# Later maxima in the second turn of a two-layer transformer kernel on Trainium2

## Chip, core and metric

The kernel runs on one core of a Trainium2 chip. Such a core has a tensor engine for matrix products (PE in the profile), a vector engine (DVE), a scalar engine for activations (ACT), a general engine (POOL, GpSimd) and a small engine that here only issues transfers (SP). Each works through a list of instructions of its own, in order, and waits on semaphores where it needs another's result. The metric is the time of one execution on the device in microseconds; lower is better.

## What is computed

Two transformer layers over an input of 8 batches, 512 tokens and 128 channels. In each, attention and a feed-forward net stand side by side on the same normalized input:

```python
xn = layernorm(x)
x  = x + attn0(xn) + ffn0(xn)    # ffn0: gate, up and down products, values rounded to fp4 by blocks of 16
xn = layernorm(x)
x  = x + attn1(xn) + moe(xn)     # moe: a shared net, and 2 of 8 experts for each token
```

Attention has 16 heads of 8 channels and a softmax over 512 keys. In both layers the kernel computes the scores twice: once roughly, for the maximum of each row, and once in full with that maximum folded in, for the exponentials.

## The kernel before

**Turns and slots.** The work on a batch is divided into turns of 16 slots. `turn_a(b)` runs layer 0's attention for batch b, `turn_b(b)` runs layer 1's attention for batch b − 1; they alternate: `turn_a(0)`, `turn_b(0)`, `turn_a(1)`, and so on. In slot k a turn computes two pairs of scores (`score_pair`, L387, lines L395) on the tensor engine, their exponentials on the scalar engine (`exponentials`, L753), and a slot later the sums with the values (`weighted_sums`, L383). All other work is hung into the slots by hand: `work_a` and `work_b` stand in each engine's program and name the slot and the place in it, "a" behind the first pair of scores, "b" behind the second, and on the vector engine "m" and "c" behind the slot's maxima.

**Maxima.** The attention of a later turn needs the maxima of its rows. They come in 16 units, u = 0 to 15. A unit is four products of `km` and `qm` on the tensor engine (L364) and two reductions of 128x1024 numbers on the vector engine (L1037). `units_a` and `units_b` (L254, L262) say which units stand in which slot; the maxima of a slot stand behind place "b" and before the sums. In `turn_a(1)` these are layer 1's maxima of batch 0, one unit a slot. Unit 4g is the first that needs group g of `qm[1]` and `km[1]` (`maxima`, L360). When units 0 to 7 are reduced, `max_rows(1, 0, 0)` turns them into rows: four transpositions (L285) into the ring, a cast on the scalar engine (L763), a subtraction on the vector engine (L1042), and on SP four small transfers (`load_rows`, L1601). The second half follows in slot 1 of the next turn.

**Banks.** All scores, maxima and some other products share three double banks (`mx`, L195, taken in turn by `to_pair`). A fourth pair waits until the first of the three before has been read. Single products and transpositions have one bank, the ring (`to_ring`), so each waits until the one before it has been copied out or read.

**What stands at the start of `turn_a(1)`.** In slot 0 place "b", `norm0(2)`; in slot 1 place "a", `max_rows(0, 1, 1)`; in slot 2, `q0(2)` at place "a" and `k0(2)` at "b" (L290). The scalar engine copies each out twice (`qk_out`, L725, lines L732 and L733), into `parts` and `qk_f`. Before that it waits until all transfers have landed that read `parts` for the batch and layer before.

**What stands at its end.** Slot 11 to 13, place "a": three groups of transpositions (`ffn_hidden`); slot 12 place "b", `gates_transposed`; slot 14 place "a", `ffn_down` (L352); slot 15 place "a", `shared_out` (L469). On the vector engine the steps of `quantize_x` stand in slots 11 to 13, and additions of the results of `ffn_down` and `shared_out` (L1031, L1130) in slots 14 and 15.

**SP's order** around the change: `store_early(1, 0)` (parts to `scratch`, L1562), `load_max(1, 0)` (`scratch` to `qm` and `km`, eight transfers, L1583), `store_late(1, 0)` (more of `scratch` and `rest`, L1568 to L1573), `load_stacks(1, 0, 0)`, `load_rows(0, 1, 1)`, `load_stacks(1, 0, 1)`, the same chain of stores and loads for layer 0's batch 2, then `load_rows(1, 0, 0)` and `load_stacks(0, 2, 0)`.

Of the kernel before, what the change touches and what calls it, by code (L numbers as in the profile page):

```python
# [28 lines left out]
SLOTS = 16  # L29
# [8 lines left out]
PLANE = B * T + 1  # L38
FIRST_TILE = 6
FIRST_UNITS = 10  # L40
NTILE = 2 * B * T // TS + E - 1
WROW = FE + EC * P + EC
NW = 4
# [46 lines left out]
def two_layers(nc, x, w_qkv, w_out0, b_out0, w_gate, w_up, w_down, wqT, wkT, wvT, woT, bq, bk, bv, bo,  # L90
               wr1, br1, wr2, br2, w1s, b1s, w2s, wmoe, b2, scratch, rest, xsort, y2, base, out):
    ctx = ExitStack()
    with ctx:
# [21 lines left out]
        iota8, ebase = sb("iota8", [P, E]), sb("ebase", [P, E])  # L115
        iota_t, token = sb("iota_t", [P, NTILE]), sb("token", [P, NT])
        minus_half = sb("minus_half", [P, NT])
# [58 lines left out]
        aside = sb("aside", [P, NTILE, 2])  # L176
        y_row = sb("y_row", [P, NTILE, 2], I32)

# [74 lines left out]

        def units_a(b, k):  # L254

            if b >= 1:
                return [(1, b - 1, k)]
            if k < SLOTS - FIRST_UNITS:
                return [(0, 0, FIRST_UNITS + k)]
            return [(0, 1, k - 8)] if k >= 8 else []  # L260
# [15 lines left out]
        def _(pe):  # L276
# [221 lines left out]
            def work_a(b, k, place):  # L498

                at = (k, place)  # L500
                if b <= LAST:
                    if at == (1 if b else 6, "a"):
                        max_rows(0, b, 1)
                    if at == (11, "a"):
                        ffn_hidden(b, 0)
                    if at == (12, "a"):
                        ffn_hidden(b, 1)
                    if at == (13, "a"):
                        ffn_hidden(b, 2)
                    if at == (14, "a"):  # L510
                        ffn_down(b)
                if 1 <= b < LAST:
                    if at == (0, "b"):
                        norm0(b + 1)
                    if at == (2, "a"):
                        q0(b + 1)
                    if at == (2, "b"):
                        k0(b + 1)
                if b >= 2:
                    if at == (3, "a"):  # L520
                        sums_transposed(1, b - 2, 0)
                    if at == (4, "a"):
                        sums_transposed(1, b - 2, 2)
                    if at == (5, "a"):
                        attention_transposed(1, b - 2)
                    if at == (6, "a"):
                        attention_out(1, b - 2)
                if b >= 1:
                    if at == (5, "b"):
                        v1(b - 1)  # L530
                    if b - 1 < LAST:
                        if at == (3, "b"):
                            router_hidden(b - 1)
                        if at == (4, "b"):
                            router_logits(b - 1)
                        if at == (10, "a"):
                            ranks(b - 1)
                        if at == (12, "b"):
                            gates_transposed(b - 1)
                    if at == (7, "b"):  # L540
                        shared_hidden(b - 1, 0)
                    if at == (8, "b"):
                        shared_hidden(b - 1, 1)
                    if at == (9, "a"):
                        max_rows(1, b - 1, 0)
                    if at == (15, "a"):
                        shared_out(b - 1)
# [112 lines left out]
            quantized_x(0)  # L660
            for u in range(FIRST_UNITS):
                if u == 1:
# [42 lines left out]
        def _(act):  # L705
# [78 lines left out]
            def work_a(b, k, place):  # L784
                at = (k, place)
                if b <= LAST:
                    if at == (1 if b else 6, "a"):
                        max_rows(0, b, 1)
                    if at == (8, "b"):
                        sums_out(0, b, 0)  # L790
                    if at == (11, "a"):
                        copy_out(("hT", b, 0), hqT[:, 0, :])
                    if at == (12, "a"):
                        copy_out(("hT", b, 1), hqT[:, 1, :])
                    if at == (13, "a"):
                        copy_out(("hT", b, 2), hqT[0:FC[2][1], 2, :], rows=FC[2][1])
                if 1 <= b < LAST:
                    if at == (0, "b"):
                        copy_out(("xT0", b + 1), xnT[0][:, :])
                    if at == (2, "a"):  # L800
                        qk_out(0, b + 1, 0)
                    if at == (2, "b"):
                        qk_out(0, b + 1, 1)
                if b >= 2:
                    if at == (0, "b"):
                        sums_out(1, b - 2, 1)
                    if at == (5, "a"):
                        copy_out(("aT", 1, b - 2), attT[:, :])
                if b >= 1:
                    if b - 1 < LAST:  # L810
                        if at == (3, "b"):
                            router_hidden(b - 1)
                        if at == (6, "a"):
                            router_exp(b - 1)
                        if at == (9, "b"):
                            router_tanh(b - 1)
                        if at == (12, "b"):
                            copy_out(("wT", b - 1), w9T[:, :], rows=E + 1)
                    if at == (7, "b"):
                        shared_hidden(b - 1, 0)  # L820
                    if at == (8, "b"):
                        shared_hidden(b - 1, 1)
                    if at == (9, "a"):
                        max_rows(1, b - 1, 0)

            def work_b(b, k, place):
# [96 lines left out]
        def _(dve):  # L923
# [286 lines left out]
            def work_a(b, k, place):  # L1210

                at = (k, place)
                if b <= LAST:
                    if at == (1 if b else 6, "a"):
                        max_rows(0, b, 1)
                    if at == (5, "c"):
                        quantize_h(b, 1, 0)
                    if at == (6, "m"):
                        quantize_h(b, 1, 1)
                    if at == (7, "m"):  # L1220
                        quantize_h(b, 1, 2)
                    if at == (7, "c"):
                        quantize_h(b, 1, 3)
                    if at == (14, "a"):
                        ffn_down(b)
                if 1 <= b < LAST:
                    if at == (4, "c"):
                        split_second(0, b + 1)
                    if at == (5, "m"):
                        split_third()  # L1230
                if b + 1 <= LAST:
                    if at == (11, "c"):
                        quantize_x(b + 1, 0)
                    if at == (12, "m"):
                        quantize_x(b + 1, 1)
                    if at == (12, "c"):
                        quantize_x(b + 1, 2)
                    if at == (13, "m"):
                        quantize_x(b + 1, 3)
                if b >= 2:  # L1240
                    if at == (3, "a"):
                        sums_divided(1, b - 2, 0)
                    if at == (4, "a"):
                        sums_divided(1, b - 2, 2)
                    if at == (6, "a"):
                        add_projection(1, b - 2)
                if b >= 1:
                    if at == (5, "b"):
                        values1(b - 1)
                    if b - 1 < LAST:  # L1250
                        if at == (4, "b"):
                            router_sort(b - 1)
                        if at == (6, "c"):
                            router_choice(b - 1)
                        if at == (8, "m"):
                            router_hits(b - 1)
                        if at == (8, "c"):
                            gate_difference(b - 1)
                        if at == (10, "b"):
                            places(b - 1)  # L1260
                        if at == (11, "m"):
                            router_weights(b - 1)
                    if at == (9, "a"):
                        max_rows(1, b - 1, 0)
                    if at == (15, "a"):
                        shared_out(b - 1)
# [107 lines left out]
            for n in (1, 2):  # L1374
                dve.drain()
                quantize_weights(n)
            for u in range(FIRST_UNITS):
                if u == 6:
# [384 lines left out]
```

## Time and profile before

| | |
|---|---|
| median of 3 runs | 1481.52 us (1475.12 to 1487.46) |
| the profiled execution | 1481.92 us |
| its span, first to last instruction | 1480.2 us |
| mean granted clock of the tensor engine | 0.906 of 2.4 GHz |

The profile is one execution. It gives each instruction its start, its duration and its line; where an engine stood idle before an instruction, it names what ended the wait. A page sums this up for the whole span. A table of waits adds up who waited for whom in a stretch; a timeline lists the instructions of an engine in order, neighbours of one kind merged (x2, x4), with the idle time before them in square brackets; a table of windows gives for chosen stretches each engine's busy time and the granted clock.

### The profile page before, as it was taken

The page shows a single profiled execution, that of the slowest core. Times are in us where ns is not written, and L with a number is a line of the kernel's source. Part 1 is how long each engine was busy: PE and PEld are TensorE (multiplying, and loading weights), DVE is VectorE, ACT ScalarE, POOL GpSimd, SP SyncE. Part 2 cuts the span into 40 slices and gives each one's busy share as a digit, 9 for nine tenths or more (in the row PEclk, how much of TensorE's full clock was granted, in tenths as well). Part 3 has the DMA queues.
Part 4 walks back from the last instruction along what each step waited for, and adds up shares of the span by engine and source line. Part 5 has one row for each costly group of instructions (what it writes and reads, how often), then busy time and mean ns, then how long its engine had stood idle before and what let it go on. Part 6 is the DMA issues. An engine that isn't in the chain of part 4 may idle for free.

```text
span 1480.2 us, 19496 instructions
## 1 busy us (share of the span) xinstructions
PE 1173.5 (79%) x6807; PEld 513.0 (35%) x6807; DVE 949.7 (64%) x1600; ACT 789.5 (53%) x1011; POOL 454.5 (31%) x409
## 2 busy tenths in 40 slices
PE   2588588887988798779877987798789746988895
PEld 1213224322432243124322431243124224778841
DVE  7857576787677767776777677767784353622323
ACT  1254265766476657665666576657666512233364
POOL 9621424232423232223222322231221211344420
PEclk9768798999799999988998999989989857999997
DMA  5512172136213611351145113511420074455544
GB/s 156 127 54 48 44 187 74 33 92 160 60 33 93 172 47 34 117 148 48 34 114 150 48 34 111 146 48 33 115 52 14 21 187 115 145 171 177 178 147 128
DMA packets 149507, 144.12 MB, mean 97 GB/s; under 512 B 13689, under 2 KB 141890, under 8 KB 149410
## 3 DMA queue, kind: packets, MB, share of 16 engines
q1 hardware_dynamic: 143922, 132.96, 33.2%
q0 software_dynamic: 4544, 9.38, 2.0%
q8 instruction: 54, 0.88, 0.3%
q10 hardware_dynamic: 944, 0.54, 0.1%
q14 instruction: 43, 0.35, 0.1%
HBM read 90.19 MB, written 52.12 MB: 96 GB/s over the span
## 4 chain that ended last, share of the span: by engine, by line
PE 40%; DVE 19%; ACT 13%; DMA 7%; issue 6%; DVEq 5%; SPq 5%; POOL 2%; ACTq 0%; POOLq 0%
DVE nm L1037 13%; PE sums L383 8%; PE mx L395 7%; ACT ex L753 5%; PE mx L364 5%; PE mx L485 3%; PE mx L494 3%; PE ring L290 2%; PE ring L295 2%; ACT L753 2%; PE ring L469 2%; DMA ks<-xsort 2%; DVEq L971 1%; DMA qs<-xsort 1%; PE ring L285 1%
## 5 line engine op out<-in xcount | busy, mean ns | idle before, releaser
L1037 DVE TENSOR_REDUCE nm<-mx 128x2 f32<-128x1024 f32 x512 | 601.7, 1216 | 165.5 <-PE mx L364 164.5
L753 ACT ACTIVATE ex<-mx 128x1024 f32<-128x1024 f32 x512 | 511.5, 1024 | 333.0 <-PE mx L395 331.6
L395 PE MATMUL mx<-qs,ks 128*128 128x512 bf16 (+1 forms) x1024 | 324.6, 414 | 73.6 <-DVE nm L1037 29.2
L383 PE MATMUL sums<-ex,vs 128*18 128x512 f32 x2048 | 295.1, 649 | 1.7 <-ACT ex L753 1.5
L395 PEld LDWEIGHTS mx<-qs,ks 128*128 128x128 bf16 (+1 forms) x1024 | 76.4, 101 | 369.4 <-issue 157.1
L364 PE MATMUL mx<-km,qm 32*128 32x512 bf16 x1024 | 143.8, 418 | 59.2 <-DVE nm L1037 26.8
L1445 POOL TENSOR_TENSOR parts<-qk_f,parts 128x512 bf16<-128x512 f32 x32 | 36.9, 1175 | 293.5 <-DVE parts L956 293.5
L1453 POOL TENSOR_SCALAR binade<-binade 128x704 f32<-128x704 f32 (+1 forms) x24 | 56.3, 2347 | 198.5 <-DVE binade L988 198.5
L364 PEld LDWEIGHTS mx<-km,qm 32*128 32x128 bf16 x1024 | 36.9, 93 | 207.3 <-issue 91.5
L1416 POOL TENSOR_TENSOR rstd<-veps,minus_half 128x4 f32<-128x4 f32 x16 | 16.8, 1047 | 247.8 <-DVE veps L947 247.8
L1478 POOL DMA_INDIRECT xsort<-xn,pos_i x64 | 62.6, 978 | 63.7 <-DVE pos_i L1124 46.5
L1485 POOL DMA_INDIRECT y<-qs,y_row x40 | 38.3, 957 | 107.8 <-DVE qs L1184 100.6
L383 PEld LDWEIGHTS sums<-ex,vs 128*18 128x18 f32 x2048 | 35.5, 98 | 74.7 <-issue 63.6
L753 ACT ACT_TABLE_LOAD x29 | 37.2, 1283 | 37.9 <-PE mx L395 37.9
L1456 POOL TENSOR_TENSOR h_sb<-h_sb,binade 128x704 f32<-128x704 f32 x32 | 53.5, 1672 | 2.6
L1485 POOL DMA_INDIRECT y<-ks,y_row x38 | 36.4, 957 | 49.9 <-DVE ks L1184 44.1
L1042 DVE TENSOR_TENSOR nm_hl<-ring,nm_hl 8x512 bf16<-8x512 f32 x32 | 22.2, 695 | 42.6 <-ACT nm_hl L763 42.6
L780 ACT ACTIVATE work<-mx,qs 128x256 f32<-128x256 f32 x40 | 15.7, 474 | 52.2 <-PE mx L485 52.2
L445 PE MATMUL mx<-xnT,w_sb 128*128 128x512 f32 x64 | 33.4, 648 | 5.3 <-DVE nm L1037 5.2
L469 PE MATMUL ring<-w_sb,hs 128*128 128x128 f32 x256 | 36.2, 285 | 0.0
L1184 DVE COPY qs<-mx 128x256 f32<-128x256 f32 x20 | 8.5, 425 | 42.3 <-PE mx L494 42.3
L757 ACT COPY pv_sb<-sums 128x512 f32<-128x512 f32 x32 | 18.7, 586 | 30.5 <-PE sums L383 30.0
(212 smaller groups left out, 1569.5 us busy)
## 6 DMA issues: line engine op xcount, KB each, us to landing
scratch<-parts SPq DMA_DIRECT2D x128, 256.0 KB, 3.7
ks<-scratch SPq DMA_DIRECT2D x64, 256.0 KB
qs<-scratch SPq DMA_DIRECT2D x64, 256.0 KB
qs<-wmoe SPq DMA_DIRECT2D x20, 514.0 KB, 3.7
ks<-wmoe SPq DMA_DIRECT2D x19, 514.0 KB, 3.6
qm<-scratch SPq DMA_DIRECT2D x64, 128.0 KB, 2.6
km<-scratch SPq DMA_DIRECT2D x64, 128.0 KB, 2.6
rest<-parts SPq DMA_DIRECT2D x32, 128.0 KB, 3.3
```

The costliest lines, as they stand in the source:

```text
L364: done = pe.matmul(bank[:, j, :], qm[l][r, g, t * P:(t + 1) * P], km[l][r, g, :], start=True, stop=True)
L383: done = pe.matmul(acc[32 * j:32 * j + 2 * VW, :], values[:, start:start + 2 * VW], ex[:, s % NEX, j, :], start=q == 0 and t == 0, stop=q ...
L395: done = pe.matmul(bank[:, j, :], ks[l][r, h, t * P:(t + 1) * P], qs[l][r, h, :], start=True, stop=True)
L469: pe.matmul(bank[:, t * P:(t + 1) * P], hs[:, c, t * P:(t + 1) * P], w2_sb[:, c, :], start=c == 0, stop=False)
L485: done = pe.matmul(bank[:, c // 2, c % 2 * TS:(c % 2 + 1) * TS], wbuf[i % NW][:, c * P:(c + 1) * P], xgT[i % 2], start=True, stop=True)
L494: done = pe.matmul(bank[:, 0, h * P:(h + 1) * P], hm[i % 2][:, c, h * P:(h + 1) * P], wbuf[i % NW][:, FE + c * P:FE + (c + 1) * P], start= ...
L753: act.activation(ex[:, s % NEX, 2 * i:2 * i + 2, :], bank[:, :, :], ACT.Exp, scale=SCALE).then_inc(free, 1)
L1037: dve.tensor_reduce(nm[l][:, t, h:h + 2], bank[:, :, :], AX.X, ALU.max, negate=True).then_inc(free, 1)
L1453: pool.tensor_scalar(e2d, e2d, 1.0, 1.5 * 2.0 ** 22, ALU.max, ALU.mult).then_inc(rounded, 1)
L1456: pool.tensor_tensor(d, d, e2d, op).then_inc(rounded, 1)
L1478: pool.indirect_dma_start(out=xsort[:, :], out_offset=bass.IndirectOffsetOnAxis(ap=pos_i[:, b, c, t:t + 1], axis=0), in_=xn[1][:, t, :], i ...
L1485: pool.indirect_dma_start(out=y2[:, :], out_offset=bass.IndirectOffsetOnAxis(ap=y_row[:, i, h:h + 1], axis=0), in_=yo[i % 2][:, h * P:(h + ...
```

## The change

In `turn_a(1)` the units start in slot 3 instead of slot 0. Slots 3 to 12 have one unit each (0 to 9), slots 13, 14 and 15 two each (10 and 11, 12 and 13, 14 and 15). Unit 7 now stands in slot 10, so `max_rows(1, 0, 0)` stands in slot 11 instead of slot 9 in the three programs that contain it (PE, ACT, DVE); in slot 11 it comes behind `ffn_hidden(1, 0)`, which has the same place. No other turn changes, and SP's and POOL's programs remain as they are.

```diff
+FIRST_SHIFT = 3
...
         def units_a(b, k):
 
+            if b == 1:
+                first, last = FIRST_SHIFT, SLOTS - FIRST_SHIFT
+                return [(1, 0, u) for u in ([k - first] if first <= k < last else [2 * k - SLOTS, 2 * k - SLOTS + 1] if k >= last else [])]
             if b >= 1:
                 return [(1, b - 1, k)]
...
-                    if at == (9, "a"):
+                    if at == (11 if b == 1 else 9, "a"):
                         max_rows(1, b - 1, 0)
```

The last two lines stand alike in the programs of the tensor, scalar and vector engine.

## Rows read from the trace of the kernel before

**Rows 1.** Page: the span; busy us, share of span, instructions of each engine.
```profile
span 1480.2 us, 19496 instructions
...
PE 1173.5 (79%) x6807; PEld 513.0 (35%) x6807; DVE 949.7 (64%) x1600; ACT 789.5 (53%) x1011; POOL 454.5 (31%) x409
```

**Rows 2.** Timeline, tensor engine, slot 0: start, us, line, count, [idle before, releaser].
```profile
184.24 0.61 PE L364 MATMUL mx<-km,qm 32*128 32x512 bf16 x4 [10.07 <-DMA km<-scratch]
```

**Rows 3.** Timeline of SP's queue: first load, first and last late stores.
```profile
180.96 0.60 SPq L1583 DMA_DIRECT2D qm<-scratch  x1
...
186.12 0.59 SPq L1568 DMA_DIRECT2D scratch<-parts  x1
...
188.32 2.00 SPq L1573 DMA_DIRECT2D rest<-parts  x2
```

**Rows 4.** Timelines of the vector and scalar engines ahead of slot 2's copies.
```profile
179.19 0.53 DVE L988 TENSOR_SCALAR binade<-h_sb 128x704 int32<-128x704 int32 x1
...
192.56 0.59 ACT L732 CAST parts<-ring 128x512 bf16<-128x512 f32 x1 [1.29 <-DMA rest<-parts]
```

**Rows 5.** Timeline of the tensor engine, slot 2: q0, k0, the unit.
```profile
189.99 1.02 PE L290 MATMUL ring<-xnT,wqkv_sb 128*128 128x512 f32 x2
...
193.69 1.13 PE L290 MATMUL ring<-xnT,wqkv_sb 128*128 128x512 f32 x2 [2.24 <-ACT qk_f L733]
194.75 0.39 PE L364 MATMUL mx<-km,qm 32*128 32x512 bf16 x4
```

**Rows 6.** Windows: stretch, length; PE, PEld, DVE, ACT, POOL; PE clock; DMA, GB/s.
```profile
76.50:86.00 9.50, 9.50 (x34) 1.60 (x32) 4.71 (x4) 4.19 (x5) 1.40 (x2) 0.50 0.18 54
...
177.00:187.00 10.00, 2.76 (x12) 1.06 (x12) 4.53 (x7) 1.17 (x3) 8.05 (x5) 0.60 0.63 187
...
193.70:200.00 6.30, 6.30 (x36) 1.40 (x36) 3.92 (x4) 4.42 (x6) 0.00 (x0) 1.00 0.78 188
```

**Rows 7.** Timeline of the scalar engine in `turn_a(0)`: exponentials of three successive slots.
```profile
85.61 1.94 ACT L753 ACTIVATE ex<-mx 128x1024 f32<-128x1024 f32 x2 [2.66 <-PE mx L395]
90.20 1.94 ACT L753 ACTIVATE ex<-mx 128x1024 f32<-128x1024 f32 x2 [2.65 <-PE mx L395]
93.28 1.94 ACT L753 ACTIVATE ex<-mx 128x1024 f32<-128x1024 f32 x2 [1.15 <-PE mx L395]
```

**Rows 8.** Timelines of three engines: slot 9's row of maxima; slots 11, 12.
```profile
225.51 1.06 PE L285 MATMUL ring<-ident,nm 128*8 128x128 f32 x4
...
228.68 0.68 DVE L1042 TENSOR_TENSOR nm_hl<-ring,nm_hl 8x512 bf16<-8x512 f32 x1 [1.88 <-ACT nm_hl L763]
...
236.84 0.66 PE L395 MATMUL mx<-qs,ks 74*128 74x512 bf16 x2
...
237.21 0.58 ACT L717 COPY hqT<-ring 128x512 f32<-128x512 f32 x1
...
237.86 2.35 DVE L1037 TENSOR_REDUCE nm<-mx 128x2 f32<-128x1024 f32 x2 [2.34 <-PE mx L364]
...
239.21 0.60 PE L285 MATMUL ring<-ident,h_sb 128*128 128x128 f32 x4
```

**Rows 9.** Timeline of the vector engine, slots 13 to 15.
```profile
246.08 2.35 DVE L1037 TENSOR_REDUCE nm<-mx 128x2 f32<-128x1024 f32 x2
...
249.45 0.69 DVE L1031 TENSOR_TENSOR acc<-acc,ring 128x512 f32<-128x512 f32 x1 [0.51 <-PE ring L352]
...
257.55 0.69 DVE L1130 TENSOR_TENSOR macc<-macc,ring 128x512 f32<-128x512 f32 x1 [4.97 <-PE ring L470]
```

**Rows 10.** Timeline of the tensor engine: slots 14, 15, and the next turn's start.
```profile
246.13 0.60 PE L395 MATMUL mx<-qs,ks 128*128 128x512 bf16 x2
246.57 2.84 PE L352 MATMUL ring<-wdT,hqT 128*128 128x128 f32 x24
...
251.09 0.61 PE L395 MATMUL mx<-qs,ks 128*128 128x512 bf16 x2
...
259.29 1.04 PE L395 MATMUL mx<-qs,ks 74*128 74x512 bf16 x4
```

More of the change, by code:

```diff
@@ L822, in work_a @@
                         shared_hidden(b - 1, 1)
-                    if at == (9, "a"):
+                    if at == (11 if b == 1 else 9, "a"):
                         max_rows(1, b - 1, 0)
@@ L1262, in work_a @@
                             router_weights(b - 1)
-                    if at == (9, "a"):
+                    if at == (11 if b == 1 else 9, "a"):
                         max_rows(1, b - 1, 0)
```

## Prediction

> **What bounds the kernel now.** I read the page first: the tensor engine is busy for 79% of the span, the vector engine for 64%, so no engine is full and the waits decide [rows 1]. Then I read the timelines of layer 0's second turn, engine by engine, for what stands idle and what ends each wait.
>
> The turn ends at 259.3 us [rows 10]. In the old order its slot 0 asks at once for layer 1's first maxima, and the tensor engine stands for 10.07 us until `km` has landed, at 184.24 [rows 2]. That is the hole the change is aimed at. But the timeline of the SP queue shows a second transfer behind the first. SP issues the early stores, then the eight loads of `qm` and `km` from 180.96, then only at 186.12 the late stores, the last two from 188.32 for 2.00 us [rows 3]. ScalarE's `qk_out(0, 2, 0)` in slot 2 waits for just these late stores, because `parts` may not be overwritten earlier. It waits 1.29 us, for `rest`, and starts at 192.56 [rows 4]. The tensor engine has issued `q0` at 189.99, and its next product of that kind, `k0` of slot 2, needs the one ring bank back: it starts at 193.69 after 2.24 us of idling [rows 5]. So two waits stand one behind the other, and the second ends 9.5 us after the first (193.7 − 184.2). In those 9.5 us the old kernel does the maxima of units 0 and 1.
>
> **The change, part by part.**
>
> *Slots 0 to 2 lose their units.* Slots 0 and 1 have scores, one transposition and the sums; nothing there waits for `km`. The vector engine is done with its own work of the turn before at 179.19 + 0.53 = 179.7 [rows 4], then does the maxima's rows of slot 1, and frees the ring at about 180.5; `q0` runs there, a good 9 us before its old 189.99. ScalarE then meets the late stores. Their time is made by the vector engine's split, GpSimd's third part and SP's own order, and none of these waits for a unit of maxima. They land at 192.5 as before, so `k0` starts at 193.7 as before. What is behind ScalarE's wait: its exponentials of slot 2's second half, its copy of `k0`, hence the ring, hence the tensor engine. The 10.07 us therefore return as a wait of about 12 us at `k0` (181.5 to 193.7). Gained is only the unit of slot 2 behind it: its four products are 0.39 us [rows 5]. I take −0.4; the bounds are 0 and −9.5 (the latter if the late stores came early, a rival below).
>
> *The clock behind the hole.* In the old trace the stretch with the 10 us hole, 177 to 187, was granted 0.60 of full speed, a mixture of 1.2 and 2.4 GHz, and 193.7 to 200 the whole 2.4 GHz [rows 6]: the slow part fell into the hole and into the products that still had the second wait before them. Now the engine stands until 193.7, and the slow part falls on slots 2 and 3, which nothing covers. What a slot costs at 1.2 GHz is shown by the turn before: at a granted 0.50 [rows 6] the exponentials of successive slots start 4.59 us apart (85.61 to 90.20), just after it 3.08 us (90.20 to 93.28) [rows 7]; 1.5 us a slot. Between no such slot and four (twice the two that fit into the 9.5 us of that stretch) I take one, +1.5; bounds 0 and +6. Of the clock the Trainium skill (TensorE: Matmul & The Clock Gate, Part 1, "What's actually happening") says that the throttled rate is the default and that activity releases it. [...] Were the rule not to hold here, the sum would be 1.5 us less, 1489.7.
>
> *Slots 3 to 12 keep one unit each*, with the same neighbours; nothing changes but the unit's number, so 0.
>
> *The row of maxima moves from slot 9 to slot 11.* In slot 9 little comes back: its four transpositions take 1.06 us [rows 8], but they lie beside exponentials which the same slot must wait for. In slot 11 they come behind `ffn_hidden`, in the same place "a", and there is one ring bank: the transpositions wait for ScalarE's copy of `hqT` (237.21 + 0.58), then take 0.60 us as the others do at 2.4 GHz, and the second pair of scores, before at 236.84, starts at about 238.3 (+1.4). ScalarE casts (0.6 us), the vector engine subtracts (0.68 us) and only then reduces the slot's unit: at about 239.8, before at 237.86, +2.0 [rows 8]. The vector engine has no idle time left in slots 12 and 13, so these 2.0 us stay. Bounds 0 and 2.3. SP issues this row's four loads two slots later, and the stacks of batch 2 queued behind them come later too; they are wanted a whole turn later, so this is free.
>
> *Slots 13 to 15 take two units each.* Three units are six reductions more; a pair of them is 2.35 us [rows 9]: 7.05 us. How much of it is hidden, step by step, with the 2.0 us carried in:
> - Slot 13: the four reductions run from 248.1 (before: two from 246.08) to 252.8. There are three double banks for scores and maxima. The first score pair of slot 14 follows four pairs of maxima and needs the bank of the second, read at 250.5; before it started at 246.13 [rows 9, 10]. +4.4.
> - Slot 14: `ffn_down` (2.84 us, from 246.57 before) ends at 253.7, its addition at 254.4; four reductions to 259.2. The first score pair of slot 15 needs the second of them, at 256.8, and follows the sums: 257.0 against 251.09, +5.9 [rows 9, 10].
> - Slot 15: `shared_out` follows, with those scores as long as before (251.1 to 257.5): to 263.4. The vector engine idled 4.97 us in front of its addition [rows 9]; slot 14's last reductions now fill half of that. The addition ends at 264.2, four reductions at 269.0.
> - Next turn: its first scores, before at 259.29 [rows 10], need the second of the four, 266.7, and the third, 267.9. GpSimd's rounding of `xq`, started 4.4 us later, is still earlier than its reader. I carry +8.2 for this part and the one before together.
>
> Bounds for the two together: if all idle time of the vector engine there were filled (0.51 + 4.97 [rows 9]), 7.05 − 5.5 = +1.6; if none, 7.05 + 2.3 = +9.4. I stay near the upper end because the order within a slot is fixed: slot 15's units stand behind `shared_out`, so they can't fill the idle time in front of it.
>
> **Sum.** −0.4 + 1.5 + 8.2 = +9.3 us. The profiled execution took 1481.92 us around a span of 1480.2 [rows 1], 0.4 us above the median of the runs (1481.52): 1481.9 + 9.3 = 1491.2, so 1491. Behind this turn every stage follows in a chain through the tensor and vector engines and begins 8 to 10 us later, and nothing gives that back.
>
> **Rivals.**
> 1. *Not slower: the tail takes the units in.* The idle time of slots 13 to 15 is filled, +1.6, with nothing for the clock: 1481.9 − 0.4 + 1.6 = 1483; with a slot 9 that gives its 1.06 us back, 1482. For it: the vector engine's 4.97 us of idle time. Against it: three banks and the fixed order. It decides if the first scores of slot 15 start less than 2 us later than before, counted from slot 3.
> 2. *Faster: the second wait isn't there.* If the late stores landed about 9.5 us earlier, `k0` would follow `q0` at once and the head gains 9.5: 1481.9 − 9.5 + 8.2 = 1481 with the full tail, 1474 with a tail of 1.6. For it: the wait seen in the old trace is only 1.29 us long. Against it: it is short because the first wait hides it; its end, 192.56, stands where SP's queue puts it.
> 3. *Slower by more: the clock.* Four slots at 1.2 GHz instead of one: 4 × 1.5 − 1.5 = 4.6 more, 1496; and if the small holes in the tail bring the low level there too, for one or two slots, 1498. For it: the hole now ends where the dense part begins. Against it: slots 3 to 8 partly wait for the vector engine, which has its own pace.
>
> **Chances.** The forecast, 1486 to 1495: 0.56. Rival 1, 1480 to 1486: 0.21. Rival 2, 1473 to 1480: 0.06. Rival 3, 1495 to 1503: 0.17. The runs of before lie between 1475.1 and 1487.5, 0.4% to either side, so about 1% is what can be told from no change: 1466.7 and 1496.3. Above 1496.3 lies most of rival 3 and the last edge of the forecast if the runs scatter upwards, 0.18. Below 1466.7 there is hardly a case, 0.03. The rest, 0.79, is within 1%. The range, 1479 to 1500, takes in rival 1 and most of rival 3 and leaves out rival 2 and the outer edges; the likeliest case's own range is 1486 to 1495.
>
> **What the profile after would show.** The wait of L364 for `km` is gone. ScalarE's wait at L732 for `rest` grows from 1.29 to some 11 us and still ends near 192.5; the tensor engine's wait at L290 grows from 2.24 to about 12 us and ends near 193.7. The granted clock behind 193.7 is below 1.0. The first scores of slot 15 and of the next turn come about 6 and 8 us later, with waits of L395 and L364 for the vector engine's L1037. It is wrong if L290's wait ends clearly before 193, or if the next turn starts within 3 us of 259.3.

## The result, and the profile after

The changed kernel takes 1497.39 us (median of 20 runs, 1485.96 to 1515.14), the kernel before 1482.87 us (20 runs, 1467.66 to 1492.82). The ratio is 1.0101, with a 95% interval of 1.0076 to 1.0126: one per cent slower, about 15 us (11 to 19). Medians take in all runs, ratios leave out those more than 1.5% above the fastest run of their kernel (three of these 20), and two of the profiled executions below, of the tail alone and of the changed kernel with another order of the stores, were such runs. The forecast was +9.3 us, 1491, within 1479 to 1500. The measured time lies in the wide range, above the 1486 to 1495 that was called likeliest: the direction and the place are right, the size is too small by a third.

The profiled execution of the changed kernel took 1492.52 us, 10.6 us more than the profiled one of before. Its page, the two lines that answer to [rows 1], shows the same busy times in a longer span:

```profile
span 1490.6 us, 19496 instructions
...
PE 1173.6 (79%) x6807; PEld 512.9 (34%) x6807; DVE 949.6 (64%) x1600; ACT 790.0 (53%) x1011; POOL 454.8 (31%) x409
```

No work was added, so all that was lost is waiting, or the tensor engine's clock. (In the changed kernel the line numbers behind `units_a` are 4 higher.) The hole first. The table of waits for 173 to 200 us (engine, line, what was waited for; us in total, times, the longest):

```profile
DVE nm L1041 <- PE mx L368: 21.2, 1, 21.2
...
PE ring L294 <- ACT qk_f L737: 12.9, 1, 12.9
ACT parts L736 <- DMA rest<-parts: 12.8, 1, 12.8
```

The wait of L364 for `km` [rows 2] is gone, and in its place stand the two that were small in [rows 4, 5]: ScalarE waits 12.8 us instead of 1.29 for the late stores, the tensor engine 12.9 us instead of 2.24 for the ring. The vector engine has nothing to reduce for 21.2 us. The tensor engine's timeline shows where the hole ends and what follows (start, us, line, count, idle time before):

```profile
177.79 1.10 PE L294 MATMUL ring<-xnT,wqkv_sb 128*128 128x512 f32 x2 [0.67 <-DVE nm_hl L1046]
178.73 0.60 PE L399 MATMUL mx<-qs,ks 74*128 74x512 bf16 x2
192.19 2.08 PE L294 MATMUL ring<-xnT,wqkv_sb 128*128 128x512 f32 x2 [12.87 <-ACT qk_f L737]
194.20 1.91 PE L387 MATMUL sums<-ex,vs 128*18 128x512 f32 x8
...
225.06 1.89 PE L399 MATMUL mx<-qs,ks 74*128 74x512 bf16 x4 [3.29 <-ACT hs L750]
...
238.30 1.01 PE L289 MATMUL ring<-ident,nm 128*8 128x128 f32 x4 [0.89 <-ACT hqT L721]
...
250.29 0.39 PE L368 MATMUL mx<-km,qm 32*128 32x512 bf16 x2 [1.00 <-ACT ex L757]
251.50 0.61 PE L368 MATMUL mx<-km,qm 32*128 32x512 bf16 x2 [0.83 <-DVE nm L1041]
252.04 1.91 PE L387 MATMUL sums<-ex,vs 128*18 128x512 f32 x8
253.89 1.03 PE L399 MATMUL mx<-qs,ks 128*128 128x512 bf16 x2
254.72 2.93 PE L356 MATMUL ring<-wdT,hqT 128*128 128x128 f32 x24
...
261.03 0.61 PE L399 MATMUL mx<-qs,ks 128*128 128x512 bf16 x2
...
270.93 0.61 PE L399 MATMUL mx<-qs,ks 74*128 74x512 bf16 x2
```

Of `q0` at 177.79 nothing is won, `k0` waits until 192.19 (193.69 in [rows 5]). `k0` then takes 2.08 us for what took 1.13, the sums 1.91 for 1.05: 1.2 GHz. The table of windows says the same of the stretches (start and end, length; PE, PEld, DVE, ACT, POOL busy; granted clock; DMA):

```profile
177.00:192.20 15.20, 1.66 (x6) 0.50 (x5) 0.65 (x2) 2.15 (x4) 7.28 (x4) 0.70 0.54 166
192.20:196.90 4.70, 4.70 (x13) 0.96 (x14) 0.00 (x0) 1.95 (x3) 0.00 (x0) 0.50 0.81 194
197.00:224.00 27.00, 20.93 (x121) 6.17 (x118) 22.24 (x40) 18.51 (x21) 6.71 (x5) 1.00 0.67 172
224.30:244.60 20.30, 17.59 (x68) 5.00 (x69) 12.67 (x24) 10.06 (x14) 10.46 (x10) 0.50 0.15 47
...
251.50:254.90 3.40, 3.40 (x13) 0.91 (x14) 3.34 (x3) 0.00 (x0) 0.00 (x0) 0.50 0.01 4
```

In [rows 6] the slow part lay in 177 to 187, and 193.7 to 200 had the full clock; now it lies behind the hole, in slots 2 and 3. And it stands twice in the tail: until 244.6, over slots 9 to 12, and from 251.5 to 254.9, in slot 13. The first of these is only partly new. The kernel before has a low stretch there too, but it ends at 237.0, early in slot 11; the 24 us from 235 on have a mean of 0.96, which is some 2 us at 1.2 GHz:

```profile
221.50:234.50 13.00, 9.60 (x41) 2.26 (x41) 10.13 (x20) 8.83 (x11) 6.02 (x5) 0.57 0.36 111
235.00:259.00 24.00, 23.05 (x164) 12.82 (x160) 14.98 (x23) 11.69 (x14) 11.99 (x11) 0.96 0.24 59
```

The vector engine in slots 11 to 15, beside [rows 8] and [rows 9]:

```profile
240.09 0.68 DVE L1046 TENSOR_TENSOR nm_hl<-ring,nm_hl 8x512 bf16<-8x512 f32 x1 [4.19 <-ACT nm_hl L767]
240.75 2.35 DVE L1041 TENSOR_REDUCE nm<-mx 128x2 f32<-128x1024 f32 x2
...
246.23 2.35 DVE L1041 TENSOR_REDUCE nm<-mx 128x2 f32<-128x1024 f32 x2 [1.55 <-PE mx L368]
...
250.23 4.61 DVE L1041 TENSOR_REDUCE nm<-mx 128x2 f32<-128x1024 f32 x4
...
257.69 0.69 DVE L1035 TENSOR_TENSOR acc<-acc,ring 128x512 f32<-128x512 f32 x1 [2.33 <-PE ring L356]
258.44 4.62 DVE L1041 TENSOR_REDUCE nm<-mx 128x2 f32<-128x1024 f32 x4
267.48 0.69 DVE L1134 TENSOR_TENSOR macc<-macc,ring 128x512 f32<-128x512 f32 x1 [4.42 <-PE ring L474]
268.35 4.62 DVE L1041 TENSOR_REDUCE nm<-mx 128x2 f32<-128x1024 f32 x4 [0.18 <-PE mx L368]
```

The twos stand there as groups of four reductions, 4.6 us each. In slot 11 the engine waits 4.19 us for the cast of the moved row; in front of the addition of `shared_out` it still waits 4.42 us, of 4.97 before.

To compare executions, the rest uses one ruler. A turn's length is counted from the end of the vector engine's split in the turn before (L956 of the kernel before; it lets the stores start) to the first exponential of the next turn's slot 1; within it, the start of ScalarE's copy of `q0` of batch 2 (L732, ended by the late stores' landing) and the first exponentials of the slots. All but the split's end are starts in the timelines of the vector and the scalar engine. The split's end differs by up to 5.9 us between the traces (169.9 to 175.8), from the first turns, which no kernel here changes; the ruler takes that out. From the copy of `q0` on:

| us | before | after | lost |
|---|---|---|---|
| copy of `q0` to slot 3 | 192.56 to 196.76: 4.20 | 191.07 to 197.13: 6.06 | 1.9 |
| slot 3 to slot 11 | to 236.29: 39.53 | to 236.66: 39.53 | 0.0 |
| slot 11 to 13 (moved row) | to 243.66: 7.37 | to 247.81: 11.15 | 3.8 |
| slot 13 to 14 | to 246.84: 3.18 | to 255.02: 7.21 | 4.0 |
| slot 14 to 15 | to 251.79: 4.95 | to 261.73: 6.71 | 1.8 |
| slot 15 to the next turn's slot 1 | to 263.47: 11.68 | to 275.52: 13.79 | 2.1 |
| sum | 70.91 | 84.45 | 13.5 |

13.5 us lost where 9.3 were forecast. Counted from the split it is 87.7 and 102.4, 14.7 us: in this execution the first loads were also issued 1.1 us later behind the split (6.4 us behind it, 5.2 before), which the other traces with this head and the old order of the stores don't show.

### The profile page after: what moved, and what is told of

It is laid out like the page before. It is cut to its first block, busy times and chain, and to the rows that moved or that the text cites. A ratio compares the mean times of both kernels' runs of the same rounds, so it can differ in the third digit from the quotient of the medians.

```text
span 1490.6 us, 19496 instructions
## 1 busy us (share of the span) xinstructions
PE 1173.6 (79%) x6807; PEld 512.9 (34%) x6807; DVE 949.6 (64%) x1600; ACT 790.0 (53%) x1011; POOL 454.8 (31%) x409
## 4 chain that ended last, share of the span: by engine, by line
PE 40%; DVE 20%; ACT 14%; issue 7%; DMA 7%; DVEq 5%; SPq 4%; POOL 2%; ACTq 0%; POOLq 0%
DVE nm L1041 14%; PE sums L387 8%; PE mx L399 7%; ACT ex L757 6%; PE mx L368 4%; PE mx L489 3%; PE mx L498 3%; PE ring L294 2%; PE ring L299 2%; DMA ks<-xsort 2%; ACT L757 2%; PE ring L473 2%; PE ring L289 1%; PE mx L449 1%; DVEq L975 1%
## 5 line engine op out<-in xcount | busy, mean ns | idle before, releaser
L294 PE MATMUL ring<-xnT,wqkv_sb 128*128 128x512 f32 x32 | 20.2, 716 | 22.1 <-ACT qk_f L737 20.7
```

Of the source, the lines that this page charges most:

```text
L294: pe.matmul(bank[0:rows, 0:width], lhsT, rhs, start=True, stop=True).then_inc(ring_full, 1)
```

## The experiments

The theory at this point had three parts: a head that only moves the hole from `km` to the late stores and pays for it with the clock; a moved row that costs 2 us or more; twos in the tail that cost the most. Its rivals were that one part, the head with its hole and clock above all, makes the whole loss. All ratios are to runs of the kernel before on the same chip; "turn" is the length by the ruler above, 87.7 us before.

### The row of maxima alone

```diff
-                    if at == (9, "a"):
+                    if at == (11 if b == 1 else 9, "a"):
                         max_rows(1, b - 1, 0)
```

> Only the row of maxima moves, from slot 9 to slot 11; the units stay one a slot from slot 0. Theory (three parts: a head that gains nothing, rows of maxima that cost 2 us in slot 11, twos in the tail that cost the most): slot 12's first scores come 1.5 to 4 us later against slot 10's than before, the whole is 1 to 4 us slower than before. Rival (the row's move makes most of the loss, because it holds the ring and the vector engine in a full slot): 8 to 12 us slower.

Measured: 1491.3 us, ratio 1.0048 (1.0015 to 1.0081). By this ratio the whole is 7 us slower (2 to 12): more than the theory said, less than the rival, and too wide an interval to choose. The turn chooses. It is 90.45 us, 2.7 longer, of which 1.97 lie between slots 11 and 13 (9.34 us for 7.37); the other 0.8 lie ahead of the copy of `q0`, where nothing was changed, and from slot 13 on all is as before. The vector and the tensor engine there:

```profile
238.35 0.60 PE L285 MATMUL ring<-ident,nm 128*8 128x128 f32 x4 [1.17 <-ACT hqT L717]
...
239.72 0.68 DVE L1042 TENSOR_TENSOR nm_hl<-ring,nm_hl 8x512 bf16<-8x512 f32 x1 [3.77 <-ACT nm_hl L763]
240.33 2.33 DVE L1037 TENSOR_REDUCE nm<-mx 128x2 f32<-128x1024 f32 x2
```

The transpositions wait for the copy of `hqT`, as reckoned, and the slot's unit starts 3.62 us behind the slot's first exponential (240.33 to 236.71) instead of 1.57 (237.86 to 236.29), 2.0 us later. The term of +2.0 us holds for the row alone. In the changed kernel the same stretch lost 3.8: there the four transpositions ran at 1.2 GHz, 1.01 us instead of 0.60, and the scores and sums up to slot 12 with them (the 224.3 to 244.6 window). That the clock makes the difference is seen in the other traces that have the row in slot 11: with the tail alone and with the stores' order changed the transpositions take 0.60 us and the stretch loses 1.97 too; with the hole filled it is at 1.2 GHz until 239.2, 7.9 us into slot 11, and loses 3.8.

### The head alone, with the twos early

```diff
+            if b == 1 and k < 6:
+                return [(1, 0, u) for u in ([2 * k - 6, 2 * k - 5] if k >= 3 else [])]
             if b >= 1:
                 return [(1, b - 1, k)]
```

> The head of the change without its tail: no units in slots 0 to 2, two each in slots 3, 4 and 5, one each from slot 6 on, the row of maxima in slot 9 as before. Theory (the head moves the hole to k0 and gains nothing; what costs is the tail's position): k0's wait at the ring is 12 to 13 us as in the changed kernel, the last slots are as before, the whole is 3 to 8 us slower than before. Rival (the loss comes with the hole at k0 and the low clock behind it, wherever the twos stand): 12 to 16 us slower, as the change itself.

Measured: 1499.62 us, ratio 1.0110 (1.0060 to 1.0160), 16 us slower, and that is what the rival said. The turn is 99.0 us, 11.3 longer; slots 11 to the next turn are as before to 0.02 us, so the whole loss lies between the copy of `q0` and slot 11. `k0` waited 11.78 us. The clock stayed low for much longer than in the changed kernel (the wait, then two windows):

```profile
187.92 2.07 PE L292 MATMUL ring<-xnT,wqkv_sb 128*128 128x512 f32 x2 [11.78 <-ACT qk_f L735]
...
177.00:187.90 10.90, 0.00 (x0) 0.00 (x0) 0.00 (x0) 1.11 (x3) 4.32 (x3) 0.50 0.70 209
188.00:200.80 12.80, 11.57 (x34) 2.01 (x36) 4.62 (x4) 4.48 (x6) 0.00 (x0) 0.50 0.81 174
```

So twos aren't cheap in early slots either, or the clock made it. The next two tell these apart.

### The hole filled

In slot 2 of the changed kernel, ahead of `k0`:

```diff
+            def fill():
+                bank, full = to_pair("fill")
+                r, h = score_rows(0), head(0, 2)
+                for n in range(48):
+                    done = pe.matmul(bank[:, n % 2, :], ks[0][r, h, 0:P], qs[0][r, h, :], start=True, stop=True)
+                done.then_inc(full, 1)
...
                    if at == (2, "b"):
+                        if b == 1:
+                            fill()
                         k0(b + 1)
```

(A copy on the vector engine that reads the bank is left out here; nothing uses its result.)

> The changed kernel with 48 extra products (bf16, 128x512, into a double bank that nobody else needs just then) on the tensor engine in the hole ahead of k0 of slot 2; their result is read by one tiny copy and not used. Theory (the hole at k0 costs twice: the wait itself, and 1.2 GHz in the slots behind it): k0 starts when it did against the stores' landing, runs at 2.4 GHz (1.05 us instead of 2.08), slot 3 starts 1.5 to 5 us earlier against it, and the whole is 2 to 5 us faster than the changed kernel. Rival (the low clock behind the hole is hidden by the vector engine's pace): 0 to 1 us.

Measured: 1500.3 us, ratio 1.0126 (1.0075 to 1.0176). In the trace:

```profile
177.22 10.52 PE L311 MATMUL mx<-qs,ks 74*128 74x512 bf16 x48
189.05 1.13 PE L294 MATMUL ring<-xnT,wqkv_sb 128*128 128x512 f32 x2 [1.30 <-ACT qk_f L746]
190.11 1.05 PE L394 MATMUL sums<-ex,vs 128*18 128x512 f32 x8
```

`k0` and the sums run at full clock, and from the copy of `q0` to slot 3 it takes 3.87 us (187.92 to 191.79): 2.2 less than in the changed kernel, and 0.33 less than before, which is the unit that slot 2 no longer has. This isolates the clock's price at this place, 2.2 us, and confirms the −0.4 of the sum. The tail, from slot 11 on, loses 11.6 us, as in the changed kernel (11.7). The time of the whole doesn't show the 2.2 us, and the 2 to 5 us of the theory aren't there: 2.2 us are 0.15%, less than half of the interval's half-width, and the whole can't decide on it.

The same filling in the kernel with the early twos:

> The kernel with the twos in slots 3 to 5 and the row of maxima in slot 9 (no units in slots 0 to 2), with the 48 extra products in the hole ahead of k0; their result is not used. Theory (of the 11 us that this kernel's turn lost against the stores' landing, the low clock behind the hole made some 3 to 5, the twos' vector work the rest): k0, the sums and the scores of slots 3 to 5 run at 2.4 GHz, the turn loses 6 to 8 us, the whole is 5 to 9 us slower than before. Rival (the twos alone make it, through banks and the vector engine): 10 to 12 us lost in the turn, clock or not.

Measured: 1494.27 us, ratio 1.0047 (1.0010 to 1.0083); the turn is 94.65 us, 6.9 longer, against 11.3 without the filling. From `q0`'s copy on it lost 82.13 − 77.85 = 4.3 us less. So the twos in slots 3 to 5 cost 7.3 us (slot 3 to 11 takes 46.80 us for 39.53), about three units of 2.35 us unhidden. The clock was full behind the hole until 204.5, where a stretch at 1.2 GHz to 207.9 began, in slots 4 and 5; what that adds wasn't separated. And the low clock behind an unfilled hole cost 4.3 us there and 2.2 in the changed kernel. The rival of the second experiment was right on its number, for two causes that add up.

### The tail alone

Units 0 to 2 in slots 0 to 2, none in slots 3 to 5, 3 to 9 in slots 6 to 12, then twos; the row in slot 11. In `units_a`, in place of the changed kernel's two lines:

```diff
+                if k < FIRST_SHIFT:
+                    return [(1, 0, k)]
+                first, last = 2 * FIRST_SHIFT, SLOTS - FIRST_SHIFT
+                return [(1, 0, u) for u in ([k - FIRST_SHIFT] if first <= k < last else [2 * k - SLOTS, 2 * k - SLOTS + 1] if k >= last else [])]
```

> The tail of the change without its head: units 0 to 2 in slots 0 to 2 as before, none in slots 3 to 5, units 3 to 9 in slots 6 to 12, two each in slots 13 to 15, the row of maxima in slot 11. Theory (the tail makes most of the loss): from slot 11 to the next turn 9 to 12 us are lost as in the changed kernel, slots 3 to 5 give 1 to 3 us back, the whole is 6 to 11 us slower than before. Rival (the head with its hole and clock makes it): 0 to 4 us slower.

Measured: 1496.01 us, ratio 1.0037 (0.9995 to 1.0080). By the ratio that is 5.5 us, between the two forecasts, and the interval includes no difference. The turn is 94.7 us, 7.0 longer, on the theory's side. The parts: slots 3 to 11 take 36.55 us, 3.0 less than before; slots 11 to 13 lose 2.0; slot 13 to the next turn takes 27.8 us, 7.9 more than the 19.8 of before. The changed kernel loses 7.9 there too (27.7), the filled one 7.8, the next experiment's 7.9. So the twos' price in the tail is the best known number here. It has a price of the clock in it: each of the five traces with twos in the tail has a short stretch at 1.2 GHz in slot 13 or between 13 and 14, and none of the nine others has one there. A unit taken out of slots 3 to 5 is worth 1.0 us, one out of the hole a tenth of a microsecond.

### The order of the stores

In the changed kernel, layer 1's late stores of batch 0 ahead of the loads:

```diff
                 store_early(1, b)
-                load_max(1, b)
-                store_late(1, b)
+                if b == 0:
+                    store_late(1, b)
+                    load_max(1, b)
+                else:
+                    load_max(1, b)
+                    store_late(1, b)
```

> The changed kernel, with layer 1's late stores of batch 0 issued ahead of the loads of qm and km instead of behind them. Theory (the hole at k0 is SP's order: the late stores stand behind eight loads that take 5 us to issue and wait for the early stores): ScalarE's wait for rest shrinks from 12.8 us to 4 to 6 us, k0 starts 6 to 9 us earlier, the whole is 5 to 9 us faster than the changed kernel, so still 5 to 10 us slower than before. Rival (the stores land late by themselves, for instance because the transfers share the engines): the wait stays above 10 us and the time is that of the changed kernel, some 14 us slower than before.

Measured: 1490.65 us, ratio 1.0029 (0.9994 to 1.0064), 0.7% below the changed kernel's ratio; the two intervals don't meet. Against before it is 4 us slower, and the interval includes no difference. SP, ScalarE and the tensor engine:

```profile
179.01 1.00 SPq L1577 DMA_DIRECT2D rest<-parts  x2
180.05 0.60 SPq L1587 DMA_DIRECT2D qm<-scratch  x1
...
183.02 0.59 ACT L736 CAST parts<-ring 128x512 bf16<-128x512 f32 x1 [4.77 <-DMA rest<-parts]
...
184.15 2.07 PE L294 MATMUL ring<-xnT,wqkv_sb 128*128 128x512 f32 x2 [4.82 <-ACT qk_f L737]
```

The last stores are issued at 179.01 instead of 186.89, ScalarE waits 4.77 us instead of 12.82, and `k0` starts 8.04 us earlier behind the same split (184.15). The turn is 94.8 us, 7.6 shorter than the changed kernel's. So 8 of the 12.8 us at `k0` are SP's order; 4.8 us of waiting stay. The low clock stays as well: `k0` takes 2.07 us, the clock is 0.50 until 193.5, the copy of `q0` to slot 3 takes 6.10 us, and slots 3 to 11 take 41.66, 2.1 more than before. And the tail's loss remains.

The same order in the kernel before:

> The kernel before, with layer 1's late stores of batch 0 issued ahead of the loads of qm and km. Theory (in the old order the second wait is only 2.24 us at k0, and the loads' landing moves later by about what the late stores take to issue): km lands 1 to 5 us later, k0 no longer waits, the whole is within 3 us of before. Rival (the late stores are what bounds the old head as well): 5 to 8 us faster.

Measured: 1491.23 us, ratio 1.0032 (0.9997 to 1.0067). `k0` waits 0.81 us instead of 2.24, `km`'s wait grows from 10.07 to 11.47, the turn is 88.2 us, 0.5 longer; the whole can't tell, its interval includes no difference. In the old order of the units there was nothing to be had from the stores, as expected: the first wait covers them.

### Moves into the hole

Two units each in slots 0 and 1, one each in slots 2 to 5, none in slots 6 and 7:

```diff
+            if b == 1 and k < 8:
+                return [(1, 0, u) for u in ([2 * k, 2 * k + 1] if k < 2 else [k + 2] if k < 6 else [])]
```

> The reverse of the change: units 0 and 1 in slot 0, 2 and 3 in slot 1, one each in slots 2 to 5, none in slots 6 and 7, then as before. Theory (between km's landing and the late stores' the vector engine has some 4.7 us of idle time, and units done there cost nothing): k0 starts within 1 us of where it did, slots 6 and 7 are each about 1 us shorter, the whole is 1 to 5 us faster than before. Rival (four pairs of maxima on three banks push q0 and k0 out): k0 starts 2 to 4 us later, and the whole is 0 to 3 us slower.

Measured: 1486.71 us, ratio 1.0019 (0.9983 to 1.0056). The rival held: the doubled units stood behind the hole at 1.2 GHz (low until 199.0), `q0` was reached only at 192.10 and `k0` started at 195.25, 4.5 us later behind the split than before; slots 6 and 7 gave 2.5 us back, and the turn is 89.9 us, 2.2 longer. It would be 3.7 longer without slot 10, which took 3.1 us instead of 4.6 because the low clock ended at its start (at 233.1), not because of the units. The whole can't tell: its interval includes no difference.

`q0` and `k0` one slot later:

```diff
-                    if at == (2, "a"):
+                    if at == (3 if b == 1 else 2, "a"):
                         q0(b + 1)
```

(`k0` and both copies on the scalar engine alike.)

> The kernel before, with q0 and k0 of batch 2 one slot later in this turn (slot 3 instead of 2). Theory (with units 0 and 1 done, tensor and vector engine idle 2.2 and 4.7 us ahead of the late stores' landing, and unit 2 could stand there): the waits of L290 and of L732 for rest go, the turn is 1 to 4 us shorter, the whole as much faster than before. Rival (the ring: q0, k0 and the router's first product in one slot make it longer by what is gained): within 1 us of before.

Measured: 1488.84 us, ratio 1.0020 (0.9990 to 1.0050). ScalarE's wait for `rest` is gone, but slot 3 now holds `q0`, `k0` and the router's product on one ring bank, waiting 0.85 and 1.24 us; the turn is 88.5 us, 0.8 longer. The rival again, by the turn; the whole can't tell.

Both `shared_hidden` of batch 0 into slot 0, in the kernel before:

```diff
-                    if at == (7, "b"):
+                    if at == ((0, "b") if b == 1 else (7, "b")):
                         shared_hidden(b - 1, 0)
-                    if at == (8, "b"):
+                    if at == ((0, "b") if b == 1 else (8, "b")):
                         shared_hidden(b - 1, 1)
```

> The kernel before, with both shared_hidden of batch 0 in slot 0 of this turn, ahead of the first unit, instead of in slots 7 and 8. Theory (the hole in front of km is free for work that waits for nothing: four products, four activations and their table loads; what the turn lacks is not an earlier start of the maxima but something to do in the hole): slots 7 and 8 shrink from 7.4 and 9.1 us to 3 to 4 us each, km's wait shrinks to 1 to 6 us, the turn is 6 to 11 us shorter and the whole 5 to 11 us faster than before. Rival (the shared net's activations push slot 1 out, and the second wait at the late stores holds k0 anyway, so the vector engine's pace decides): within 2 us of before.

Measured: 1495.26 us, ratio 1.0062 (1.0030 to 1.0094): slower. Within the turn the move did something of what it should:

```profile
169.48 3.73 PE L445 MATMUL mx<-xnT,w_sb 128*128 128x512 f32 x8
179.66 0.61 PE L364 MATMUL mx<-km,qm 32*128 32x512 bf16 x4 [6.46 <-DMA km<-scratch]
...
222.75 0.19 PE L454 MATMUL ring<-mask,upper 128*128 128x40 bf16 x1 [4.14 <-DVE nm_hl L1042]
```

The products, eight matmul instructions, fill a third of the hole, `km`'s wait is 6.46 us, slots 7 and 8 take 8.2 us together instead of 16.5. But slots 9 and 10 grow by 4.3 us, because the vector engine's work of these slots, which the table loads of slots 7 and 8 had covered, now stands open (4.14 us in front of the ranks of the router, L454). The turn is 84.4 us, 3.3 shorter, not 6 to 11. So that the whole is 9 us slower does not come from this turn.

The same in the changed kernel:

> The changed kernel, with both shared_hidden of batch 0 in slot 0 in the same way. Theory (the hole at k0 is as free for them as the old one was; the tail's loss stays): the turn is 6 to 10 us shorter than the changed kernel's, the whole as much faster than the changed one, still 3 to 8 us slower than before. Rival (the changed kernel's head is better filled and catches up with before): as fast as the version of before with the same move.

Measured: 1498.86 us, ratio 1.0098 (1.0063 to 1.0133); the turn is 98.8 us, 3.6 shorter than in the changed kernel's trace (1.1 of it that trace's late loads) and 11.1 longer than before. Half of the theory holds (the tail's loss stays; 6 to 10 us were forecast for the head), and again there is no gain in the whole.

### An edit that does nothing

```diff
-FIRST_UNITS = 10
+FIRST_UNITS = 5 + 5
```

> The kernel before with a constant written in another way: the same instructions. It shows what an edit that does nothing measures, and how long the later turns are in another execution of the same program. Theory (the later turns' lengths, 65.8 to 68.8 us and 75.5 to 84.5 us in the traces so far for the same instructions, depend on where the clock falls to 1.2 GHz, and that varies between executions of one kernel too): the ratio's interval holds 1.0, and turns 2 to 13 show both long and short lengths, as in the other traces. Rival (the longer later turns of most edited kernels are brought about by the edits to the second turn): turns 2 to 13 are as long as in the trace of before, within 3 us in sum.

Measured: 1482.58 us, ratio 0.9988 (0.9951 to 1.0025). The turn is 87.9 us. Behind it come `turn_b(1)` to `turn_a(7)`, twelve turns whose instructions are the same in all these kernels. Their windows show (before, changed, this one, and the one with `shared_hidden` moved, in this order):

```profile
260.00:1134.80 874.80, 728.89 (x4332) 267.69 (x4330) 638.80 (x926) 547.59 (x638) 247.67 (x210) 0.94 0.31 82
```

```profile
271.60:1145.80 874.20, 726.16 (x4332) 266.85 (x4332) 639.47 (x927) 547.78 (x637) 247.85 (x210) 0.95 0.31 82
```

```profile
259.70:1127.10 867.40, 726.81 (x4332) 268.88 (x4330) 637.77 (x926) 546.70 (x638) 247.69 (x210) 0.95 0.31 83
```

```profile
252.20:1144.20 892.00, 746.25 (x4336) 270.89 (x4336) 639.31 (x926) 548.12 (x638) 247.69 (x210) 0.92 0.30 80
```

Vector and scalar engine are busy for the same time to 0.3%; the stretch lasts 867 to 892 us with the granted clock, 0.95 to 0.92. Single turns of the null edit differ from those of before by up to 5 us (`turn_a(6)` 76.7 against 81.7, `turn_b(2)` 68.3 against 65.8). The theory (it varies between executions of one kernel) is right for single turns; the sums of before and of the null edit over these twelve turns are 7.4 us apart, more than the rival's 3, but the edited kernels lie mostly above both: 881 to 892 in ten of them, 874 to 875 in the changed kernel and in the one with units put forward. For the kernel with `shared_hidden` moved the lower clock is no accident of one trace: its 12 runs have a mean clock of 0.899, the 29 of before on the same chip 0.907. These means are of the whole execution. Why the clock is lower in the twelve turns behind most of the edits is left open; no run here separates it.

## Why the prediction was right, and where it was too small

**The head gains nothing: right.** `k0` waits 12.87 us where about 12 were said, ScalarE 12.82 where 11 were said, and the wait ends by the late stores. That these are bound by SP's order is shown by the run with that order changed: the wait fell to 4.8 us. The unit of slot 2 was worth 0.33 us, the term was −0.4.

**The clock behind the hole: right in kind, and counted at one of its three places.** The term was +1.5; the filled hole shows 2.2 us. Not every wait brings the low clock: in [rows 5, 6] `k0` ran at the full one (1.13 us) behind a wait of 2.24 us. The Trainium skill (TensorE: Matmul & The Clock Gate, Part 1, "What's actually happening") says that activity releases the throttled rate; the trace agrees (1.00 behind the filled hole, 0.50 behind the unfilled one). The forecast had no such term for the tail, where it gave the low clock only to rival 3. But the moved row's stretch ran at 0.50 until 244.6, 1.8 us over the row's own price (3.8 − 2.0), and slot 13 from 251.5 to 254.9. These three places make most of the 4.2 us by which the ruler's 13.5 exceed the forecast's 9.3: 0.7 behind the hole, 1.8 in the row's stretch, 1.3 or more in slot 13 (below).

**The moved row: right.** +2.0 said, 1.97 measured alone. One sub-step was wrong: the vector engine was said to have no idle time in slots 12 and 13; in the changed kernel it waits 1.55 us in slot 12 for the unit's products, which came late at 1.2 GHz; in the two traces with the full clock there (tail alone, stores' order) it waits 0.23.

**The twos: the mechanism right, the size short.** The sum put 6.2 us behind the row's 2.0; five kernels show 7.8 to 7.9, where three units' vector work is 7.05. (By its own steps, 266.7 and 267.9 against first scores from 259.29 on, the 8.2 is the second pair of scores; the first would be 7.4.) Step by step, without the row's part: slot 13 was to lose 2.4 us (4.4 less the 2.0 carried in) and lost 4.0; slots 14 and 15 with the next turn's start were to lose 3.8 (8.2 − 4.4) and lost 3.9. The missing 1.6 us are in slot 13. The walk-through let the sums and scores run at full clock, and they took 1.91 and 1.03 us where the full clock takes 1.05 and 0.61: 1.3 us of the 1.6, read from these rows. The third pair of maxima waits 1.00 us for the exponentials of the slot's second scores before it gets a bank, which the walk-through left out, but that costs nothing here: the vector engine's four reductions run without a gap (4.61 us from 250.23), and the fourth pair, in front of the sums, waits for them. That the last steps agree to 0.1 us is in part luck. In the traces of the tail alone and of the stores' order the low stretch began 0.8 to 0.9 us later in slot 13 and reached into `ffn_down` (3.7 us instead of 2.8): there slot 13 lost 3.3 us and what follows 4.6. The sum, 7.9, is the same, and no run has the twos in the tail without a low stretch.

**The rivals.** "The tail takes the units in" needed slot 15 less than 2 us late; it was late by 9.6 counted from slot 3 (64.6 us for 55.0). "The second wait isn't there" is refuted by the wait itself. "Slower by more: the clock" is what happened in part, and the measured 1497.4 lies in its band, 1495 to 1503: the low clock stood in the tail too, as it said, though behind the hole it cost 2.2 us and not 6. (Its 4 × 1.5 − 1.5 is 4.5, not 4.6, which changes nothing.)

**The sum.** −0.3 + 2.2 + 3.8 + 7.9 = 13.6 us by the measured terms, 13.5 by the ruler, 14.5 between the medians, whose interval is far wider than these differences. That nothing gives it back held for the turns behind: the changed kernel is 12.0 us late in slot 1 of the next turn (14.7 by the ruler, less the 2.7 us that its split stood earlier), 11.2 at the start of `turn_b(2)`, 11.1 at that of `turn_b(7)`, in two traces whose later turns happened to be equally long. What the other runs lose there isn't known: the changed kernel's 20 runs have a mean granted clock of 0.903, its profiled one 0.910 and a time 5 us below their median.

## What to carry to other kernels

A wait that a trace shows as 1 us may be 13 us long behind the wait in front of it: before work is moved out of a hole, follow the queue to the next thing that the same engines wait for. Units that were nearly free in the hole (0.1 us each) cost 2.4 to 2.6 us each in the slots they were moved to, most of it because the vector engine had no room there (2.35 us of work for each). And a turn that is measured by a ruler within the trace tells about parts of 2 us that the whole kernel's time, with intervals of ±0.25 to 0.5%, can't.

## What the runs showed of the hardware that was not expected

The low clock outlasts a hole by very different times. Behind holes at the same `k0`, 12.9 and 11.8 us long, it was 0.50 for 4.7 us in one trace and for 12.8 us in the other, although the tensor engine was busy for 4.70 of 4.70 and 11.57 of 12.80 us. Behind a hole of 4.8 us, with the stores' order changed, it was 0.50 for 9.3 us (184.15 to 193.5). In these three the length of the hole told nothing of how long the low clock behind it would last.

Twelve turns of identical instructions took 867 to 892 us in fourteen traces with a granted clock of 0.95 to 0.92, and with an edit that shortened an earlier turn by 3.3 us the whole was 0.6% slower. The changed kernel's loss, as its trace shows it, is not of this kind: its twelve later turns took 874.2 us, those of before 874.8.
